# Reordering the fill and the end of a 16-batch adaLN pipeline on one core

## The reference

```
h  = layernorm(x) * (1 + ca) + sa
u, gate = split(h @ W_in.T)
b_t = u @ W_state.T
dt = min(softplus(u @ W_dt.T + b_dt), 10)
decay = exp(-dt * rate)
state[t] = decay[t] * state[t-1] + (1 - decay[t]) * b_t[t]      # scan over 512 tokens
x1 = x + ga * ((state @ W_C.T * silu(gate) + h * D) @ W_out.T)
h2 = layernorm(x1) * (1 + cb) + sb
xr, xk = mix of h2[t] and h2[t-1] with mu_r and mu_k
out = x1 + gb * (sigmoid(xr @ W_r.T) * (relu(xk @ W_k.T)**2 @ W_v.T))
```

## Time and profile before

| | |
|---|---|
| Median of 3 runs | 369.3 us (369.03 to 369.5) |
| The profiled execution's own time | 369.45 us |
| Its span | 367.7 us |
| Granted TensorE clock over the span | 0.997 |
| PE busy | 357.8 us (97%), 1672 matmuls |
| PEld busy | 272.7 us (74%) |
| DVE, ACT, POOL busy | 302.3, 306.4, 255.4 us (82%, 83%, 69%) |
| Chain that ended last | PE 87%, ACT 4%, DVE 4%, issue 2%, DMA 1%, POOL 1% |

### The profile page before, as it was taken

The page is one execution under the profiler, slowest core; times in us unless marked ns, Lnnn a source line. Parts: engine busy times, 40 slices in busy tenths (PEclk is TensorE's granted clock), DMA queues, the critical chain, the costliest instruction groups (busy, mean ns, idle before and its releaser), DMA issues.

```text
span 367.7 us, 5567 instructions
## 1 busy us (share of the span) xinstructions
PE 357.8 (97%) x1672; PEld 272.7 (74%) x1672; DVE 302.3 (82%) x638; ACT 306.4 (83%) x418; POOL 255.4 (69%) x267
## 2 busy tenths in 40 slices
PE   8999898999999999999999999999999999999995
PEld 4577566877778787777878777787877778786753
DVE  2787988988889798988979798897979879767845
...
DMA packets 19006, 29.15 MB, mean 79 GB/s; under 512 B 1184, under 2 KB 9888, under 8 KB 18848
## 3 DMA queue, kind: packets, MB, share of 16 engines
...
...
## 4 chain that ended last, share of the span: by engine, by line
PE 87%; ACT 4%; DVE 4%; issue 2%; DMA 1%; POOL 1%; ACTq 0%; SPq 0%; DVEq 0%; POOLq 0%
PE slot L244 68%; PE slot L251 8%; PE slot L340 3%; PE slot L495 2%; PE slot L489 2%; PE slot L488 2%; PE slot L258 1%; DMA w_in<-weights_in 1%; ACT prev L594 1%; PE slot L288 1%; DVE stats L788 1%; DVE wmod L850 1%; PE slot L348 1%; POOL rstd L1063 1%; DVE z L891 0%
## 5 line engine op out<-in xcount | busy, mean ns | idle before, releaser
L1063 POOL TENSOR_TENSOR rstd<-mv,half_neg 128x4 f32<-128x4 f32 x16 | 16.1, 1007 | 47.0 <-DVE mv L803 47.0
L594 ACT ACTIVATE prev<-slot,mod,mix_prev 128x512 f32<-128x512 f32 x64 | 46.3, 784 | 1.7 <-PE slot L251 1.4
L1039 POOL TENSOR_TENSOR xr_lo<-xr,xr_hi 128x512 fp32r<-128x512 f32 x32 | 42.3, 1325 | 3.5 <-ACT xr_hi L695 3.5
L244 PE MATMUL slot<-h_hi,wf_hi 128*128 128x512 f32 x120 | 43.7, 404 | 1.1 <-DVE z L891 0.8
L244 PE MATMUL slot<-h_hi,wf_lo 128*128 128x512 f32 x120 | 42.8, 397 | 0.0
L1039 POOL TENSOR_TENSOR xk_lo<-xk,xk_hi 128x512 fp32r<-128x512 f32 x30 | 38.4, 1302 | 5.7 <-ACT xk_hi L622 5.7
L1039 POOL TENSOR_TENSOR k_lo<-k_act,k_hi 128x512 fp32r<-128x512 f32 x30 | 38.1, 1290 | 5.7 <-ACT k_act L745 5.7
L1130 POOL TENSOR_TENSOR z_lo<-z,z_hi 128x512 fp32r<-128x512 f32 x26 | 33.7, 1298 | 9.9 <-ACT z_hi L679 6.7
L251 PEld LDWEIGHTS slot<-ident,xn 128*128 128x128 f32 x248 | 28.7, 141 | 10.6 <-issue 4.7
L251 PE MATMUL slot<-ident,xn 128*128 128x128 f32 x248 | 34.8, 274 | 1.7 <-DVE xn L827 1.5
L1082 POOL TENSOR_TENSOR h_lo<-h,h_hi 128x512 fp32r<-128x512 f32 x28 | 35.8, 1302 | 0.0
...
## 6 DMA issues: line engine op xcount, KB each, us to landing
...
```

The lines of the kernel that those rows point to most:

```text
L244: ins = nc.tensor.matmul(out, w[:, c, at + d * P:at + (d + 1) * P], x[:, c, :], start=first, stop=last)
L594: return nc.scalar.activation(prev[:, mix, i, 1:T + 1], ps_n[:, i, :], ACT.Identity, bias=mod_at(SHIFT2 + i, k), scale=mix_prev[:, mix, i, ...
L1039: nc.gpsimd.tensor_tensor(lo, x, hi.bitcast(F32), ALU.subtract).then_inc(done, 1)
L1063: nc.gpsimd.tensor_tensor(rstd2[:, k % 2], mv2[:, k % 2, 1, :], half_neg[:], ALU.pow).then_inc(rstd2_ok, 1)
```

## The change

It touches four places.

- **Fill.** PSUM slots are given out anew (slots 1 and 3 trade places for o, r, x1 and v; h of batch 2 gets slot 2). On TensorE `first_norm(2)` goes ahead of the gate of batch 1, the gate of batch 2 is finished before its dt and b, which go behind the transposes of xn2(0), and `token_stats(1)` moves ahead of the loop. The first norm of batch 0 signals its first four transposes separately. Three of the eight later modulation groups are computed between the two halves of the gate of batch 0. ScalarE, VectorE and GpSimd follow in their orders; the wait of `rounded_h` is on the high products of the gate alone.
- **Tokens.** The token array is laid out by partition on the host, so that one partition's data of a batch is contiguous. The tokens of batch 0 come in two transfers, the second issued by ScalarE.
- **Each step.** `xr_lo[1]` is issued ahead of the products of `state_lo`, all eight transposes of xn2 follow in one group, and `first_norm(a)` goes behind the first half of V's low part.
- **End.** The square of k of batch 14 moves behind the `prev` copies of K. For the last batch both low parts of k are made by VectorE, the residual of batch 14 is put between them, V's second output half is computed in two quarters of 256 tokens in two PSUM banks, the first half's gate is scaled by ScalarE and its residual added by GpSimd, and the last rows leave in three transfers.

```diff
 ps_front, ps_y = slot[0], slot[0]
-ps_o, ps_r = slot[1], slot[1]
-ps_n = slot[2]
+ps_n, ps_r = slot[2], slot[3]
...
+def ps_o(k):
+    return slot[1] if k < WHOLE else slot[3]
 
 def ps_h(k):
-    return slot[1] if 0 < k <= WHOLE else slot[0]
+    return slot[k] if k <= WHOLE else slot[0]
 
 
 def ps_gate(k):
     return slot[3] if k <= WHOLE else slot[2]
 
 def ps_x1(k):
-    return (slot[2] if k == 0 else slot[3] if k < LAST else slot[0])[:].rearrange("p a b -> p (a b)").rearrange("p (t c) -> p t c", t=TT)
+    return (slot[2] if k == 0 else slot[1] if k < LAST else slot[0])[:].rearrange("p a b -> p (a b)").rearrange("p (t c) -> p t c", t=TT)
 
 def ps_v(k):
-    return slot[3] if k < LAST else slot[2]
+    return slot[1] if k < LAST else slot[2]
 
 def ps_k(k):
...
+quarter = [slice(0, T // 2), slice(T // 2, T)]
+v_end = [ps_v(LAST)[:, 1, 0:T // 2], ps_v(LAST - 1)[:, 1, T // 2:]]
...
+    sp.dma_start(x_tok[:, 0, 0:TT // 2], x_tok_d[0, :, 0:TT // 2]).then_inc(s_xt[0], 16)
...
     def first_norm(k):
         pe.wait_ge(xn1a_ok, k + 1)
         pe.wait_ge(xn1b_ok, k + 1)
-        if 0 < k <= WHOLE:
-            before(pe, x1_ok[0], k - 1)
-            before(pe, x1_ok[1], k - 1)
-        else:
+        if k == WHOLE:
+            pe.wait_ge(mod_step, 2)
+        elif k > WHOLE:
             before(pe, z_ok[0], k)
             before(pe, z_ok[1], k)
         to_channels(ps_h(k), xn1).then_inc(t1_ps, 1)
...
+        if k == 0:
+            pe.wait_ge(h_ok, WHOLE + 1)
...
+    pe.wait_ge(xn1a_ok, 1)
+    pe.wait_ge(xn1b_ok, 1)
+    for c in range(CH):
+        for t in range(TT):
+            last = nc.tensor.transpose(ps_h(0)[:, c, t * P:(t + 1) * P], xn1[:, t, c * P:(c + 1) * P], ident[:])
+        last.then_inc(t1_half_ps if c == 0 else t1_ps, 1)
...
     half(g_out, w_early, GATE, h[:, 0], 0, first=True)
-    half(g_out, w_early, GATE, h[:, 0], 1, last=True).then_inc(g_ps, 1)
     pe.wait_ge(s_wmod2, 16)
     modulation(4, 3, slot[2][:, 1, :])
+    half(g_out, w_early, GATE, h[:, 0], 1, last=True).then_inc(g_ps, 1)
...
     attention_out(0, 1)
+    first_norm(2)
     gate_high(1)
     gate_low(1)
-    first_norm(2)
     token_stats(0)
     state_out(1)
     pe.wait_ge(hhi_ok, 2)
     pe.wait_ge(silu_ok, 2)
     gate_high(2)
-    pe.wait_ge(z_ok[0], 2)
-    pe.wait_ge(z_ok[1], 2)
-    front_high(2)
+    gate_low(2)
+    attention_out(1, 0)
     pe.wait_ge(xn2a_ok, 1)
     pe.wait_ge(xn2b_ok, 1)
     to_channels(ps_n, xn2).then_inc(t3_ps, 1)
+    attention_out(1, 1)
+    front_high(2)
     front_low(2)
-    gate_low(2)
-    attention_out(1, 0)
-    attention_out(1, 1)
+    token_stats(1)
...
-        if live(c) and c < LAST:
+        if 1 < c < LAST:
...
                 state_out(b)
+        if live(d) and d > 0:
+            pe.wait_ge(xrlo_ok[1], d + 1)
+            half(r_out, wl_hi, MIX_R, xr_lo, 1, last=True).then_inc(r_ps, 1)
         if split(b):
             pe.wait_ge(slo_ok, b - WHOLE + 1)
             for i in range(CH):
...
                 pe.wait_ge(relu_ok, d + 1)
             to_channels(ps_n, xn2, range(0, TT // 2))
-        if live(d):
-            pe.wait_ge(xrlo_ok[1], d + 1)
-            half(r_out, wl_hi, MIX_R, xr_lo, 1, last=True).then_inc(r_ps, 1)
         if live(c) and c < LAST:
             pe.wait_ge(xn2b_ok, c + 1)
             to_channels(ps_n, xn2, range(TT // 2, TT)).then_inc(t3_ps, 1)
+        if d == 0:
+            pe.wait_ge(xrlo_ok[1], d + 1)
+            half(r_out, wl_hi, MIX_R, xr_lo, 1, last=True).then_inc(r_ps, 1)
...
+            for j in (0,):
...
+            for q in range(2):
+                if q == 1:
+                    pe.wait_ge(x2_ok[0], d)
+                    pe.wait_ge(x2_ok[1], d)
+                at = MIX_V + P
+                for i in range(CH):
+                    nc.tensor.matmul(v_end[q], wl_hi[:, i, at:at + P], k_hi[:, i, quarter[q]], start=(i == 0), stop=False)
+                    nc.tensor.matmul(v_end[q], wl_lo[:, i, at:at + P], k_hi[:, i, quarter[q]], start=False, stop=False)
+                for i in range(CH):
+                    last = nc.tensor.matmul(v_end[q], wl_hi[:, i, at:at + P], k_lo[:, i, quarter[q]], start=False, stop=(i == CH - 1))
+                last.then_inc(v_ps, 1)
...
-        if live(a):
-            first_norm(a)
         if live(d) and d < LAST - 1:
             pe.wait_ge(klo_ok[0], d + 1)
             half(v_out(d), wl_hi, MIX_V, k_lo, 0)
+        if live(a):
+            first_norm(a)
...
+    act.dma_start(x_tok[:, 0, TT // 2:], x_tok_d[0, :, TT // 2:]).then_inc(s_xt0, 16)
...
-        before(act, g_ps, k if k > 1 else 0)
+        before(act, ghi_ps, k - 1)
...
     ln1_apply(0)
     act.wait_ge(mod1_ok, 1)
+    act.wait_ge(t1_half_ps, 1)
+    modulated(0, 0).then_inc(h0_ok, 1)
     act.wait_ge(t1_ps, 1)
-    modulated(0, 0).then_inc(h0_ok, 1)
...
@@ -648,29 +693,34 @@
     exponential(1)
     decays(1)
     nc.scalar.preload_act_table_set("silu_and_others")
-    for at in (MIX_V, OUT):
-        nc.scalar.copy(wl_hi[:, :, at:at + C], w_late[:, :, at:at + C]).then_inc(wl_hi_ok, 1)
-    act.wait_ge(s_wy, 16)
-    nc.scalar.copy(wy_hi[:], w_y).then_inc(wy_hi_ok, 1)
-    gate_silu(1)
     act.wait_ge(t1_ps, 3)
+    act.wait_ge(z_ok[0], 1)
+    act.wait_ge(z_ok[1], 1)
     modulated(2, 0)
     modulated(2, 1).then_inc(h_ok, 1)
     rounded_h(2)
+    gate_silu(1)
+    nc.scalar.copy(wl_hi[:, :, MIX_V:MIX_V + C], w_late[:, :, MIX_V:MIX_V + C]).then_inc(wl_hi_ok, 1)
+    nc.scalar.copy(wl_hi[:, :, OUT:OUT + C], w_late[:, :, OUT:OUT + C]).then_inc(wl_hi_ok, 1)
+    act.wait_ge(s_wy, 16)
+    nc.scalar.copy(wy_hi[:], w_y).then_inc(wy_hi_ok, 1)
+    gate_silu(2)
     nc.scalar.preload_act_table_set("natural_log_exp_and_others")
     ln1_apply(3)
     act.wait_ge(mix_ok, 1)
     act.wait_ge(t3_ps, 1)
     previous(KEY, 0, 0)
     previous(REC, 0, 0).then_inc(prev_ok[0], 1)
-    exponential(2)
     previous(REC, 1, 0)
     previous(KEY, 1, 0).then_inc(prev_ok[1], 1)
     rounded_xk(0, 0)
+    exponential(2)
+    rounded_xk(0, 1)
+    rounded_xr(0, 0)
     decays(2)
-    rounded_xk(0, 1)
+    rounded_xr(0, 1)
     nc.scalar.preload_act_table_set("silu_and_others")
-    gate_silu(2)
+    rounded_state(2)
...
+        if split(b) and b > WHOLE:
+            rounded_state(b)
...
-            before(act, v_ps, d)
             if d < LAST:
+                before(act, v_ps, d)
                 nc.scalar.activation(k_hi[:], k_act[:], ACT.Square).then_inc(khi_ok, 1)
             else:
                 for i in range(CH):
                     act.wait_ge(k_half_ps if i == 0 else k_ps, 1 if i == 0 else d + 1)
                     nc.scalar.activation(k_act[:, i], ps_k(d)[:, i], ACT.Relu).then_inc(half_relu_ok[i], 1)
                     act.wait_ge(half_relu_ok[i], 1)
+                    act.wait_ge(v_ps, d)
...
-        if live(d) and d < LAST:
+        if live(d) and c < LAST:
             nc.scalar.activation(k_act[:], k_act[:], ACT.Square).then_inc(kact_ok, 1)
-        if live(d) and c < LAST or d == LAST:
...
+            act.wait_ge(r_ps, d + 1)
+            before(act, rv_ok, d)
+            nc.scalar.activation(r_gate[:, 0], ps_r[:, 0], ACT.Tanh, scale=0.5).then_inc(tanh_ok, 1)
+            act.wait_ge(tanh_ok, d + 1)
+            nc.scalar.activation(r_last[:], r_gate[:, 0], ACT.Identity, bias=mod_at(GATE2, d), scale=mod_at(GATE2, d)).then_inc(scaled_ok, 1)
+            nc.scalar.activation(r_gate[:, 1], ps_r[:, 1], ACT.Tanh, scale=0.5).then_inc(tanh_ok, 1)
+            act.wait_ge(x2_ok[1], d + 2)
+            act.dma_start(out_d[d, P:, quarter[1]], x2[:, d % 2, 1, quarter[1]]).then_inc(s_out[d % 2], 16)
...
             previous(KEY, 1, c).then_inc(prev_ok[1], 1)
+            nc.scalar.activation(k_act[:], k_act[:], ACT.Square).then_inc(kact_ok, 1)
...
     ln1_stats(4)
-    ln1_mean_variance(4)
     ln1_apply(3)
     mixing(0, 0)
+    after_attention(1)
+    mixing(0, 1)
     clipped(2)
-    mixing(0, 1)
-    after_attention(1)
+    after_transpose(1)
     driven(2)
     scanned(2)
-    after_transpose(1)
+    normalised(1)
+    ln1_mean_variance(4)
 
...
-        if live(c):
+        if live(c) and c > 1:
...
-            for i in (1,):
+            before(dve, s_out[(d - 1) % 2], 16 * ((d - 1) // 2))
+            for i in range(CH):
                 dve.wait_ge(half_k_ok[i], 1)
                 dve.wait_ge(khi_half_ok[i], 1)
                 dve.wait_ge(v_ps, d)
                 nc.vector.tensor_tensor(k_lo[:, i], k_act[:, i], k_hi[:, i].bitcast(F32), ALU.subtract).then_inc(klo_ok[i], 1)
-            dve.wait_ge(tanh_ok, d + 1)
+                dve.wait_ge(rv_ok, d)
+                residual(d - 1, i)
+            dve.wait_ge(scaled_ok, 1)
             dve.wait_ge(s_out[d % 2], 16 * (d // 2))
-            for i, v_done in ((0, v_half_ps), (1, v_ps)):
-                dve.wait_ge(v_done, 1 if i == 0 else d + 1)
```

(32 more changed lines are left out.)

76 lines of the change are left out of this document (44 added, 32 removed).

## The result

| | before | after |
|---|---|---|
| median of 4 runs each | 369.38 us (369.03 to 369.5) | 363.02 us (362.19 to 364.53) |
| profiled execution, its span | 369.45, 367.7 us | 362.19, 360.4 us |
| granted TensorE clock over the span | 0.997 | 1.000 |
| DMA packets over the span, all queues | 19006 | 13150 |

The ratio is 0.9827, with a 95% interval of 0.981 to 0.984: 6.4 us faster. Forecast were 362.7 us and a chance of 0.91 for faster. The profiled execution after is the fastest of its four, so the 7.3 us between the two spans is more than the 6.4 us between the medians; where such a difference can come from is told with the end.

The account below looks back on a forecast made before the run. TensorE was taken to set the pace of the steps. Start 0.3, fill 1.7, steps 3.5, steps 16 and 17 0.2 and end 1.1 sum to 6.8 off the profiled 369.45: 362.7 us, range 361.2 to 366.4.

Parts of the forecast that it names:

- Steps: Twelve like steps, s = 4 .. 15: 0.29 us gained in each, 3.5 us in all (2.4 to 3.7).
- bound of 0.31: Each step: upper bound of the gain, the lower being 0.20, where the tanh's gain does not reach K.
- The margin named for `k_lo[0]`: Each step: 0.3 of margin before a later k_lo[0] makes the kernel slower; slower had a chance of 0.05.
- Fill: From 31.64 to K of batch 1: the new order gains 1.7 us (0.5 to 2.7).
- new waits of 2.3: Fill: xn2(0) 0.5, x1 of batch 1 0.3, mixes 0.45, xr_lo[0] 0.3, k_lo[0] 0.55, with small restarts 2.3.
- the old 4.0: Fill of the kernel before, 31.64 to 66.24: TensorE's work is 30.6 of 34.6, so 4.0 is waiting.
- Start: Start of the kernel, up to the front product at 12.28: gain 0.3 us (0 to 0.5).
- the wait for h: Start: h's first pair needs only four transposes, whose last starts some 0.48 sooner; the second half also comes in time.
- The token halves land while TensorE is busy: Start: the tokens land during weight products and the first modulation, up to 10.1, so their edit was priced at nothing.
- End: Last batch: no stall at k_lo[1], V's second half in quarters, shorter VectorE tail; gain 1.1 us (0.4 to 1.4).
- Steps 16 and 17: One transpose group less in step 16 (0.1), K copies of prev ahead of a square in step 17 (0.1): 0.2.
- the first rival: The steps keep their period, as the later y eats what the earlier R gives: 366.2 us, chance 0.14.

Follow-up runs that it names:

- a_filler: The changed kernel with one more GpSimd subtraction of 128x256, output unread, ahead of k_lo in every step: 365.95 us, ratio 0.990.
- a_table: The changed kernel with ScalarE's table load between batch 1's decay and h of batch 2 moved behind the rounding of h: 362.43 us.
- a_table_klo: As a_table, and GpSimd makes k_lo[0] of batch 0 ahead of ln1_scale(4): 362.01 us, ratio 0.9792.
- a_again: The changed kernel, nothing altered, run once more beside the last experiments: 362.98 us, ratio 0.9825.
- a_oldtok: The changed kernel with the tokens as before (old layout, one transfer for batch 0): 363.38 us, ratio 0.9827.
- b_fn: The kernel before with first_norm(a) moved behind k_lo[0] and nothing else: 369.83 us, ratio 1.0016.
- b_steps: The kernel before with both step edits alone (xr_lo[1] ahead of state_lo, first_norm(a) behind V's first low half): 365.29 us, ratio 0.9875.
- b_tokens: The kernel before with the tokens' edit alone (layout by partition and two transfers for batch 0): 369.18 us, ratio 0.9984.
- b_layout: The kernel before with the new token layout alone, still one transfer: 369.35 us, ratio 0.9992.
- b_end: The kernel before with the edits of the last batch and of batch 14's square alone: 368.4 us, ratio 0.9973.

## Why the prediction was right, and where its terms were off

**Steps.** The mechanism is shown, edit by edit: R's early end costs z 0.27, and the later `first_norm` gives it back. The term was 0.29 a step; it measured 21.19 - 20.83 = 0.36, and 4.25 / 12 = 0.354 over all of them. The missing 0.06 to 0.07 is the first K pair: the gap from its start to the next falls from 0.53 (214.50 to 215.03) to 0.46 (189.35 to 189.81), the restart behind a wait, which the prediction's bound of 0.31 left out. The margin named for `k_lo[0]`, 0.3, measured 0.3 in a_filler.

**Fill.** This is the step that failed in size: 0.54 instead of 1.7. The prediction listed new waits of 2.3. Measured by starts, with the undisturbed distances from the same trace or from a_table:

| wait | forecast | measured | how |
|---|---|---|---|
| token_stats(0) | 0 | 0.2 | 34.16 against 33.98 |
| z of batch 1 | 0 | 0.75 | 1.69 against 0.94 |
| xn2 of batch 0 | 0.5 | 0.8 | 2.47 against 1.71 (28.58 to 30.29) |
| x1 of batch 1, xr_lo[0] | 0.6 | 0.15 | 1.00 and 0.56 against 0.94 and 0.47 |
| mixes of batch 0 | 0.45 | 0.85 | 49.96 against 48.30 + 0.79 |
| k_lo[0] of batch 0 | 0.55 | 0.7 | 60.59 against 59.42 + 0.47 |

They sum to 3.4 in place of 2.3 (listed: 2.1 and small restarts), and of the old 4.0 some 0.6 is then saved; measured were 0.54. L852 is the largest part of it: with its block at 0.43 in place of 1.00 and the pair 0.7 earlier, a_table has K of batch 1 0.76 sooner behind the first front product (52.58 against 53.34), of the 1.2 that were missing. The rest is spread over the waits of the table and not traced to one cause. The sentence that failed is "I laid the new order down from 31.64 with the durations the same instructions have in the trace": a duration is not a property of the instruction alone. The same operation had lasted 0.17 at this place in the kernel before (L795, at 37.84), with GpSimd idle from 35.51 to 38.62, and the change put GpSimd's pair there. The trace of before held the warning, in the 1.07 at 55.17. The Trainium skill ("SBUF — State Buffer", SBUF: two separate sides) has the rule: VectorE and GpSimd share a pair of ports, and a VectorE operation with two SBUF inputs and a GpSimd operation that reads SBUF lock each other out for a whole instruction. The traces agree: 1.00, 0.43, 0.35 and 1.07, each ending within 0.03 of a GpSimd subtraction, and 0.17 with GpSimd idle.

**Start.** 1.26 instead of 0.3. The term that was priced, the wait for h, was right: from the warm-ups to the front product 1.19 (11.09 to 12.28) became 0.86 (10.16 to 11.02), 0.33. What was priced at nothing was not nothing: the token pieces. "The token halves land while TensorE is busy" looked at who waits for the tokens, not at what lies behind them on the same queue: the weights landed 0.52 earlier (6.11 to 5.59). Another 0.52 lies between the starts of the weights' product and the modulation, 2.37 (6.11 to 8.48) against 1.85 (5.59 to 7.44). In the kernel before the first three products of the eight run slowly, 0.59, 0.42 and 0.28 from start to start against 0.32, 0.22 and 0.21 after, at a granted clock of 1.00 in both; a_table_klo has it too (2.36 in all, a_again and a_table 1.83), and its cause is open. But without this slowness the kernel before would have gained little: in a_oldtok, b_fn and b_steps, all with the old tokens, these products run at full pace and TensorE then waits 0.44 to 0.54 for the modulation's weights, which start it at 8.32 to 8.63. So the modulation's weights are behind the tokens in the same queue too, and their landing (6.3 to 6.8 us after issue without the layout, 5.6 to 6.5 with it) sets this stretch as well; how much of the 0.52 that makes is not shown, since it scatters between executions. The modulation behind it took 0.10 longer: 0.33 + 0.52 + 0.52 - 0.10 = 1.27. The advice of the Trainium skill ("DMA: Bandwidth & Descriptors", Rules for kernel authors) is on transfers to disjoint halves of the partitions; the halves here are of tokens, over all partitions, so only its reason, the shared engines, bears on them. Nothing was found against it: b_tokens, with the split, starts the weights' product at 5.72, b_layout, without it, at 5.67. The prediction took from it that the whole token edit is worth 0, but the edit is also a layout, on which that rule says nothing.

**End.** 1.07 against 1.1. The stall at `k_lo[1]` is gone: V's first half takes 1.40 (353.65 to 355.05) and not 2.10 (359.88 to 361.98), the 0.7 that was forecast. The last VectorE pass ends at 357.84, 2.56 ahead of the end, as forecast. With the slow landing of a_again the same stretch is 8.4 us long and the gain is gone, so the 1.07 holds for executions that land like the profiled one; b_end's median, 1.2 below the runs beside it, suggests that most do.

**Steps 16 and 17** gave 0.1 of 0.2. The forecast sum of 6.8 came close to the 7.3 measured because the start gave 1.0 more and the steps 0.75 more, while the fill gave 1.2 less: the sum was better than its terms, and that is luck. Two small slips stand in the prediction: without the gain of the steps its sum is 366.2, as in the first rival, and not 366.3, and the work of the fill adds up to 30.5, not 30.6.
